# A graph layer and an attention-gated mixture on one core: GpSimd not drained between stages, destination terms first, 28 early scatters, four landing semaphores, earlier blocks

## The reference

```
x = x + gnn(layernorm(x))        # 200000 edges, sorted by destination
x = x + ffn(layernorm(x))
gnn: msgs = features[src] * edge_weight;  agg = segment_sum(msgs, dst);  agg @ W.T + b
ffn: h = (x @ W_gat) as (nodes, 4 heads, 4 experts)
     131072 edges and one loop per node:
     e = leaky_relu(a_src[src] + a_dst[dst], 0.2);  alpha = softmax of e over the edges of a destination
     agg = segment_sum(h[src] * alpha) + b_gat
     scores = layernorm(agg) * gamma + beta, mean over heads;  top 2 of 4, softmax -> gates g
     out = sum over experts of g[e] * (gelu(x @ W1[e] + b1[e]) @ W2[e] + b2[e])
```

## Time and profile before

| | |
|---|---|
| median of 3 runs | 3775.73 us (3775.3 to 3779.75) |
| profiled execution: its own time | 3777.66 us |
| profiled execution: span | 3775.6 us |
| TensorE busy | 2982.2 us (79%) |
| GpSimd busy | 2745.2 us (73%) |
| VectorE busy | 1982.0 us (52%) |
| ScalarE busy | 823.6 us (22%) |
| mean granted TensorE clock | 0.895 of full speed |

### The profile page before, as it was taken

One profiled execution on the slowest core, in us unless ns is written; L12 is line 12 of the kernel. 1 busy time (PEld: TensorE's weight loads), 2 busy tenths in 40 slices (PEclk: granted clock), 3 DMA queues, 4 the chain that ended last, 5 costly groups with the idle time before them and its releaser, 6 DMA issues. The chain is left out here.

```text
span 3775.6 us, 58501 instructions
## 1 busy us (share of the span) xinstructions
PE 2982.2 (79%) x13925; PEld 2434.1 (64%) x13926; DVE 1982.0 (52%) x5026; ACT 823.6 (22%) x2338; POOL 2745.2 (73%) x2817
## 2 busy tenths in 40 slices
PE   1465566576867898878888799999999999997348
PEld 1354444454645666666666688888888888886337
DVE  8676667877777666564344223333342434241557
ACT  6300000000111111111222222223232322221147
POOL 6477777777777777777777677777777777777572
PEclk6687778787878999999999899999999999998679
DMA  9533333333333444444444122232222222221279
GB/s 350 175 104 102 105 108 109 106 110 112 113 111 113 120 123 123 123 120 124 128 129 128 47 73 56 55 115 58 71 55 74 56 73 72 54 74 36 65 264 365
DMA packets 276541, 424.61 MB, mean 112 GB/s; under 512 B 59704, under 2 KB 210211, under 8 KB 275363
## 3 DMA queue, kind: packets, MB, share of 16 engines
q0 software_dynamic: 114208, 216.64, 21.7%
q1 hardware_dynamic: 64175, 114.71, 8.3%
q10 hardware_dynamic: 98004, 91.50, 7.5%
HBM read 317.12 MB, written 105.97 MB: 112 GB/s over the span
## 5 line engine op out<-in xcount | busy, mean ns | idle before, releaser
L653 POOL DMA_INDIRECT rows<-feats,src_t x1500 | 1475.0, 983 | 485.3 <-issue 442.2
L1166 POOL DMA_INDIRECT got<-row_dram,src_sorted x1024 | 997.4, 974 | 332.9 <-issue 332.9
L812 PE MATMUL node_sums<-rows,ys_ahead 128*128 x3904 | 995.9, 409 | 285.7 <-SPq L636 133.8
L812 PEld LDWEIGHTS node_sums<-rows,ys_ahead 128*128 128x128 f32 x3904 | 763.8, 202 | 485.5 <-issue 371.1
L1249 PE MATMUL d_hidden<-d_yt,w 128*128 128x256 f32 x3136 | 714.1, 381 | 35.2 <-DVE d_yt L1333 35.2
L1260 PE MATMUL d_expert<-w,hid 128*128 128x256 f32 x3136 | 708.7, 379 | 0.0
L1249 PEld LDWEIGHTS d_hidden<-d_yt,w 128*128 128x128 f32 x3136 | 595.5, 191 | 116.0 <-DVE d_yt L1333 36.0
L1260 PEld LDWEIGHTS d_expert<-w,hid 128*128 128x128 f32 x3136 | 595.8, 190 | 81.0
L1312 DVE TENSOR_TENSOR yo<-d_expert,x_and_b 128x512 f32<-128x512 f32 x196 | 135.5, 692 | 880.2 <-PE d_expert L1260 872.4
L871 DVE TENSOR_SCALAR ys_ahead<-iota,rel,ew_t 128x128 f32<-128x128 f32 x1952 | 558.4, 363 | 64.4 <-DVE rel L867 0.5
L1194 ACT ACTIVATE hid<-d_hidden,b1c 128x256 f32<-128x256 f32 x784 | 326.3, 471 | 1020.1 <-PE d_hidden L1249 845.2
(11 more groups left out here) (303 smaller groups left out, 2185.0 us busy)
## 6 DMA issues: line engine op xcount, KB each, us to landing
y_dram<-yo ACTq DMA_DIRECT2D x196, 256.0 KB, 2.3
ys<-y_dram SPq DMA_DIRECT2D x36, 1024.0 KB, 9.1
rows<-feats,src_t POOLq DMA_INDIRECT x1500, 2.8
got<-row_dram,src_sorted POOLq DMA_INDIRECT x1024
ys_ahead<-y_dram SPq DMA_DIRECT2D x13, 1024.0 KB, 11.0
x_dram<-edge_plan ACTq DMA_DIRECT2D x98, 128.0 KB
d_x<-x_dram ACTq DMA_DIRECT2D x49, 256.0 KB, 2.9
ys_ahead<-in_x ACTq DMA_DIRECT2D x97, 128.0 KB
```

The lines of the kernel that those rows point to most:

```text
L653: pool.indirect_dma_start(rows[:, g % RING, j, :], None, feats, bass.IndirectOffsetOnAxis(ap=m.src_t[:, g * GT + j:g * GT + j + 1], axis=0 ...
L812: t = pe.matmul(psA[:, ds(((code >> 1) & 1) * 512, FEAT)], hot[:, r, j, :], rows[:, ds((code >> 2) & (RING - 1), 1), j, :], start=False, s ...
L1166: pool.indirect_dma_start(got[:, k, j, 0:ROWF], None, m.row_dram, bass.IndirectOffsetOnAxis(ap=m.src_sorted[:, BEGIN[b] + j:BEGIN[b] + j + ...
```

## The change

Five things. The blocks of stages 1 to 3 are made with `no_gpsimd_drain=True`: GpSimd has no drain at their end. In `terms`, the destination terms come first; both kinds of terms are now made of the unscaled numbers and then scaled by 1/std, the scaling of the 16 numbers comes before the second `s_row`, and the shift comes last; SP stores `adst_dram` before `row_dram`, and GpSimd waits for `s_row` of 1. `SPREAD_BEFORE` is 28. `BLOCK_PAIR` has six blocks one pair earlier, the seventh stays at 47. Each buffer has four semaphores, one for each 35 columns of a block, and `maxima` waits for each that the block reaches.

```diff
-SPREAD_BEFORE = 22
+SPREAD_BEFORE = 28
-BLOCK_PAIR = [11, 17, 23, 30, 36, 42, 47]
+BLOCK_PAIR = [10, 16, 22, 29, 35, 41, 47]
...
-        block = ctx.enter_context(nc.Block())
+        block = ctx.enter_context(nc.Block(no_gpsimd_drain=True))
...
-                for n, (d, t) in enumerate(((m.row_dram, m.node_row), (m.adst_dram, m.node_dst))):
+                for n, (d, t) in enumerate(((m.adst_dram, m.node_dst), (m.row_dram, m.node_row))):
...
-            pool.wait_ge(s_row, 2)
+            pool.wait_ge(s_row, 1)
...
-                c.inc(v.scalar_tensor_tensor(m.shift[:, a:b], m.mean[:, a:b], -1.0, m.rstd[:, a:b], ALU.mult, ALU.mult))
-                c.done(v.tensor_tensor(m.node_row[:, a:b, 0:HE], m.node_row[:, a:b, 0:HE],
-                                       m.rstd[:, a:b, None].to_broadcast([P, n, HE]), ALU.mult))
-                for k, o in enumerate((m.node_row[:, a:b, HE:ROWF], m.node_dst[:, a:b, :])):
+                by_rstd = lambda w: m.rstd[:, a:b, None].to_broadcast([P, n, w])
+                for k, o in ((1, m.node_dst[:, a:b, :]), (0, m.node_row[:, a:b, HE:ROWF])):
                     c.done(v.tensor_tensor(prod[:, 0:n, :], m.node_row[:, a:b, 0:HE],
                                            att[:, k:k + 1, :].to_broadcast([P, n, HE]), ALU.mult))
                     c.done(v.tensor_reduce(o, prod[:, 0:n, :].rearrange("p t (h e) -> p t h e", e=EXPERTS), AX_X,
                                            ALU.add))
+                    c.done(v.tensor_tensor(o, o, by_rstd(HEADS), ALU.mult))
+                    if k == 0:
+                        c.done(v.tensor_tensor(m.node_row[:, a:b, 0:HE], m.node_row[:, a:b, 0:HE], by_rstd(HE),
+                                               ALU.mult))
                     v.sem_inc(s_row, 1)
+                c.done(v.scalar_tensor_tensor(m.shift[:, a:b], m.mean[:, a:b], -1.0, m.rstd[:, a:b], ALU.mult, ALU.mult))
...
-        s_got = [sem(f"d_gathered{k}") for k in range(NBUF)]
+        QUARTER = BLOCK // 4
+        s_got = [[sem(f"d_gathered{k}_{q}") for q in range(4)] for k in range(NBUF)]
+        in_quarter = lambda b, q: max(0, min(size(b), (q + 1) * QUARTER) - q * QUARTER)
...
-                                            ).then_inc(s_got[k], 16)
+                                            ).then_inc(s_got[k][j // QUARTER], 16)
...
-                v.wait_ge(s_got[b % NBUF], 16 * sum(size(a) for a in range(b % NBUF, b + 1, NBUF)))
+                for q in range(4):
+                    if in_quarter(b, q):
+                        v.wait_ge(s_got[b % NBUF][q], 16 * sum(in_quarter(a, q) for a in range(b % NBUF, b + 1, NBUF)))
```

## The result

The changed kernel takes 3743.34 us (median of 4 runs, 3737.3 to 3745.49), the kernel before 3775.74 in the runs beside it. The ratio is 0.991, with a 95% interval of 0.9895 to 0.9925: faster by 32.4 us. The forecast was 3759.1, in a range from 3755 to 3767, so the sign was right and the gain is nearly twice what was forecast. The profiled execution took 3742.51 us, its span is 3740.8.

A forecast was written before the change was run, and what follows sets the result against it. GpSimd's string (wait for terms, 98 scatters, 1024 gathers) was taken to bound the kernel, TensorE having slack. 4.65 + 6.35 + 5.8 - 0.15 = 16.65 us off the median 3775.73 gave 3759.1, range 3755 to 3767.

The forecast's parts named there:

- Wait for the terms: End of stage 2: reordered attention terms let GpSimd's first scatter start earlier, at 2075.75; gain 4.65 us.
- 28 scatters and the missing drain: Barrier between stages 2 and 3: 28 early scatters and no GpSimd drain (some 6.4 us) there; gain 6.35 us.
- the stated upper bound: Barrier between stages 2 and 3: it does not wait for the last scatter to end; 1.0 us more gain.
- that the six scatters are made before is not a gain by itself: Barrier between stages 2 and 3: GpSimd makes 98 scatters either way; six moved earlier only keep it busy up to the barrier.
- The third drain: End of the expert stage: without GpSimd's drain the next stage's first issue comes earlier; gain 5.8 us, bounds 0 and 6.5.
- The rival built on idle times that are no drain: Barriers: idle time is no drain or the argument drops nothing; only the terms' 4.65 remain, 3771.1 us; chance 0.10.
- the one in which only one drain pays: Barriers behind stages 2 and 3: only one drain's removal pays, 5.8 or 6.35 us lost, 3765.2 us; chance 0.10.
- Blocks a pair sooner: Expert stage: six blocks taken one pair earlier turn one long TensorE stall into three; gain 0.
- The stalls forecast at 9, 14 and 17 us: Expert stage: VectorE's idle time before blocks, waiting for gathers, at pairs 22, 41 and 47.
- Four semaphores: Expert stage: up to three more waits per block on VectorE, one on the path at block 7; costs 0.15 us.
- nothing stops the gathers: Expert stage: GpSimd's 1024 gathers run from 2217.9 to 3547.0 us, median 0.947 us each, without being stopped.
- Slower, by TensorE's clock: Expert stage: TensorE stays at 1.2 GHz after pair 41's stall, 28 us more per pair; eight pairs 3954 us; chance 0.03.

The follow-up runs named there:

- e15: Changed kernel with 22 early scatters instead of 28, at clock 0.89: 3748.7 us, ratio 0.9921 to the kernel before.
- e7: Kernel before with only GpSimd's drains at the ends of stages 1 to 3 taken out: 3762.69 us, ratio 0.9973.
- e16: Changed kernel with the block pairs of before (11, 17, 23, 30, 36, 42, 47), at clock 0.89: 3742.23 us, ratio 0.9907.
- e6: Changed kernel with one landing semaphore per buffer again, all else changed: 3760.08 us, ratio 0.9958 to the kernel before.
- e5: Kernel before with four landing semaphores per buffer and nothing else, at clock 0.89: 3756.33 us, ratio 0.9953.
- e3: Changed kernel with two semaphores per buffer, gathers split differently in each block; no time given, pauses behind the 133rd gather in block 3, 139th in block 5.
- e11: Changed kernel with two landing semaphores per buffer (70 columns each) instead of four, at clock 0.73: ratio 0.9952 to the kernel before.
- e14: Changed kernel with one semaphore per buffer and GpSimd waiting for landings in the middle of blocks 1, 3 and 5: 3774.48 us, one run.
- e1: Kernel before with four landing semaphores per buffer and nothing else, at clock 0.74: ratio 1.0012.
- e8: Changed kernel with 22 early scatters instead of 28, at clock 0.74: ratio 0.9947 to the kernel before.
- e10: Changed kernel with the block pairs of before, at clock 0.74: ratio 0.9953 to the kernel before.
- e12: Changed kernel with the block pairs of before, run again at clock 0.73: ratio 0.996 to the kernel before.

## Why the forecast had the sign and half the gain

*Wait for the terms (4.65).* The size was right: measured 4.69 on GpSimd's start. But e15 shows that this is worth little alone: with 22 scatters the first gather, counted from the reciprocal, comes at 142.88 us, against 143.77 in e7, which has the old terms. The barrier, not the terms, held the string. The early terms count because six more scatters fill the time that they free. So the term was right as a shift of GpSimd's start, but it is not a gain that could be had by itself. (These are single executions, good to some 2 us.)

*28 scatters and the missing drain (6.35).* The first gather came 11.9 us earlier, 10.6 from the reciprocal on, where 11.0 was summed. The sum had GpSimd's 29th scatter 1.36 us behind the end of the 28th; it came 0.31 behind it, which is the stated upper bound: the barrier did not wait for the scatters but hung on SP's store. Slower scatters took more than that back: the first and the third lasted 1.70 and 2.23 us, and the 98 took 2.8 us more than at 1.281 each. That the total came out near is in part luck. Split by e7 and e15: drain 4.0, terms 0.9, six scatters 5.8. The prediction's drain of 6.4 us was there, but only 4.65 of it were in reach, since SP's last store holds the barrier up to 1.94 us behind its issue (e7). The prediction's "that the six scatters are made before is not a gain by itself" holds for the sum as it was made, but with 22 the barrier hangs on SP's store and GpSimd idles 5.4 us: the six are what fills that time.

*The third drain (5.8).* Measured 6.23 and, alone in e7, 6.22. The Trainium skill's page "VectorE: DVE Perf Modes", section "The DRAIN you can't avoid", gives some 12 ns for the drains that stand before and after a kernel's own work. GpSimd's drain at the end of a block is not one of these: it cost 6.22 us here, and the measurement decides. The rival built on idle times that are no drain falls by e7, and so does the one in which only one drain pays: both do, with 3.71 and 6.22 us.

*Blocks a pair sooner (0).* Right (e16). The stalls forecast at 9, 14 and 17 us are 0, 1.5 and 12.3 in the changed kernel, since the gathers come sooner than I had them; in e6, without the semaphores, they are 8.5, 12.2 and 14.8.

*Four semaphores (-0.15).* This step failed. It priced only VectorE's side, the waits, by the 0.15 us before a product. And it rested on the reading that nothing stops the gathers, which is false: seven pauses do. On GpSimd's side, where each gather signals the semaphore, the row was in front of me: 332.9 us of idle time for 1024 gathers at 0.30 us each is 26 too many, of which the pauses are 21, and I asked only what had slowed the gathers' mean. Measured: 19.3 us for the semaphores alone (e5), and 16.7 between e6 and the changed kernel (3760.08 less 3743.34). With the pauses in place of the 0.15, the sum is 16.8 + 20.9 = 37.7, against 34.8 between the two profiled spans and 32.4 between the medians; gathers that took 3.7 us more in all (1001.1 against 997.4) are most of the difference to the spans. Why a row of signals to one semaphore makes GpSimd pause stays open.

*Slower, by TensorE's clock.* TensorE did fall to 1.2 GHz after the stall of 8.00 us: the next 16 matmuls took 6.58 us. But the 16 after them took 3.62 again, as in the earlier trace rows, so the loss that this rival needs was not seen.

## What to carry to other kernels

Multiply the usual gap by the count in the bounding engine's group, and look for whatever is left over before pricing any edit: here 21 of the 26 us left over in one row were worth more than everything that the prediction had costed. Where a change edits what an instruction signals, price the side that raises the semaphore too. And a barrier opens with its last arrival: in these runs GpSimd's drain was dear only where GpSimd arrived last, and scatters moved ahead of the barrier paid because GpSimd would have stood idle there.

## What the hardware showed that I had not expected

- GpSimd pauses 3.1 to 4.0 us, mostly 3.2, before the 114th indirect gather in a row that raises one semaphore, for gathers of 128 or 120 rows; before the 128th for 112 rows; before the 129th for 96, 64 or 32 rows. Changing to another semaphore after 20 or more gathers starts the count anew (e3, e5, e11), a wait for the landing does not (e14). What is behind it is open, as is the shorter pause of 1.78 us with alternating semaphores.
- GpSimd's drain at a block's end runs some 7 us behind its last scatter. It cost 6.2 us where nothing covered it, 3.7 to 4.65 where it began with SP's last store, 0.75 where it began 4.6 us before that store, and nothing where it began 6.0 before it (e1).
- Without a drain, a barrier does not hold back for GpSimd's scatters, ended or not: the 29th follows the 28th after 0.31 us, and in e6 another engine's next stage began 1.80 us before the 28th did.
- At a mean granted clock of 0.73 to 0.74, near variants of the changed kernel (22 scatters, old pairs, two semaphores: e8, e10, e11, e12) gain 0.4 to 0.5%, about half of its 0.9% at 0.89; the changed kernel itself was not run there. In these runs TensorE pauses between expert matmuls for nothing that the profile names (1068 us of idle time in e1), and GpSimd waits for buffers.
